# Hypergraph block on one core: second batch's degrees and B stage ahead of the first W2 stage, zero matmuls ahead of the first A, edge means ahead of z

## The reference

```python
h = relu(layernorm(x))                       # 1024 x 256
H = (adj != 0);  w = adj[0, :]               # incidence; first row = hyperedge weights
Dn = 1 / (H @ w);  Be = 1 / H.sum(axis=0)    # node degrees, edge counts (0 where empty)
z = relu(Dn * (H @ (Be * (H.T @ (h @ W1.T)))) + b1)
z = layernorm(z) * gamma + beta              # 1024 x 512
y = Dn * (H @ (Be * (H.T @ (z @ W2.T)))) + b2
out = x + (y + h)
```

## Time and profile before

| | us |
|---|---|
| median of 3 runs | 637.7 (637.48 to 640.55) |
| the profiled execution's own time | 639.25 |
| its span, first to last instruction | 637.4 |
| busy: PE / DVE / ACT / POOL | 620.3 / 473.3 / 290.9 / 111.6 |
| mean granted TensorE clock | 0.997 |

### The profile page before, as it was taken

One profiled execution on the slowest core, in us unless ns is written; L12 is line 12 of the kernel. 1 busy time (PEld: TensorE's weight loads), 2 busy tenths in 40 slices (PEclk: granted clock), 3 DMA queues, 4 the chain that ended last, 5 costly groups with the idle time before them and its releaser, 6 DMA issues.

```text
span 637.4 us, 11994 instructions
## 1 busy us (share of the span) xinstructions
PE 620.3 (97%) x4808; PEld 467.7 (73%) x4808; DVE 473.3 (74%) x1148; ACT 290.9 (46%) x540; POOL 111.6 (18%) x132
## 2 busy tenths in 40 slices
PE   2999899999999999999999999999999999999998
PEld 2756758688586885778766886768858688586887
DVE  6999878976599665995779948798478876388632
ACT  4476743463435535364353632646334363125620
POOL 0115029230310304004040040401212012000000
PEclk9999989999999999999999999999999999999999
DMA  8995870069800697109940099203990159000701
GB/s 336 260 348 105 143 320 4 31 144 179 339 34 1 160 201 301 34 1 204 258 201 34 26 222 299 116 34 84 205 364 10 34 111 213 9 1 2 197 3 67
DMA packets 146215, 89.78 MB, mean 141 GB/s; under 512 B 134896, under 2 KB 135536, under 8 KB 141168
## 3 DMA queue, kind: packets, MB, share of 16 engines
q1 hardware_dynamic: 146160, 89.02, 51.8%
HBM read 47.06 MB, written 8.39 MB: 87 GB/s over the span
## 4 chain that ended last, share of the span: by engine, by line
PE 90%; DVE 6%; ACT 2%; DMA 1%; issue 0%
PE acc L583 18%; PE acc L600 18%; PE acc L523 15%; PE acc L564 12%; PE acc L544 11%; PE acc L503 7%; PE acc L505 7%; PE acc L485 2%; DVE z L940 1%; DMA z<-z_split_ring 1%; DVE incidence L876 1%; DVE stat L945 1%; DMA x_in<-x 1%; ACT z L673 1%; ACT z_split_ring L672 1%; ACT residual L649 1%
## 5 line engine op out<-in xcount | busy, mean ns | idle before, releaser
L583 PE MATMUL acc<-xw_split,incidence 128*128 128x256 f16 x1024 | 113.2, 273 | 0.0
L600 PE MATMUL acc<-edge_means,incidence_t 128*128 128x256 f16 x1024 | 113.1, 273 | 0.0
L583 PEld LDWEIGHTS acc<-xw_split,incidence 128*128 128x128 bf16 x1024 | 100.1, 98 | 13.2 <-DVE xw_split L976 0.2
L600 PEld LDWEIGHTS acc<-edge_means,incidence_t 128*128 128x128 bf16 x1024 | 100.2, 98 | 13.1
L630 ACT ACTIVATE edge_means<-acc,edge_inverse 128x256 f16<-128x256 f32 x128 | 55.4, 474 | 116.8 <-PE acc L583 69.9
L503 PE MATMUL acc<-h_split,incidence 128*128 128x257 f16 x448 | 98.6, 273 | 0.0
L505 PE MATMUL acc<-h_split,incidence 128*128 128x256 f16 x448 | 98.6, 273 | 0.0
L523 PE MATMUL acc<-incidence_t,edge_means 128*128 128x512 bf16 x448 | 97.8, 379 | 0.0
L564 PE MATMUL acc<-w_split,z 128*128 128x256 f16 x768 | 87.2, 276 | 2.2 <-DMA z<-z_split_ring 2.2
L564 PEld LDWEIGHTS acc<-w_split,z 128*128 128x128 f16 x768 | 75.8, 99 | 12.3 <-issue 2.5
L544 PE MATMUL acc<-w_split,pt_split 128*128 128x512 f16 x384 | 84.2, 379 | 0.0
(11 more groups left out here) (104 smaller groups left out, 636.9 us busy)
## 6 DMA issues: line engine op xcount, KB each, us to landing
adj_in<-adj SPq DMA_DIRECT2D x32, 1024.0 KB, 10.4
out<-residual SPq DMA_DIRECT2D x32, 256.0 KB, 2.6
x_in<-x SPq DMA_DIRECT2D x7, 1024.0 KB, 5.5
edge_weights<-adj SPq DMA_DIRECT2D x7, 512.0 KB, 3.7
x_in<-x SPq DMA_DIRECT2D x2, 512.0 KB, 4.5
z<-w1t SPq DMA_DIRECT2D x1, 512.0 KB, 12.5
xw_split<-w2t SPq DMA_DIRECT2D x1, 512.0 KB, 13.3
incidence_t<-incidence SPq DMA_TRANSPOSE x32, 4.9
```

Of the source, the lines that this page charges most:

```text
L583: last = nc.tensor.matmul(acc[:, 0:DOUT], inc[:, b.slot, ct, P * et:P * (et + 1)], xw[:, ct, part, :], start=(ct == 0 and part == HI), sto ...
L600: last = nc.tensor.matmul(acc[:, 0:DOUT], inc_t[:, b.slot, ct, et, :], edge[:, et, part, :], start=(et == 0 and part == HI), stop=(et == T ...
```

## The change

Five edits, all in the opening; the loop from its second pass on is unchanged.

1. `keep_busy`: POOL clears the high half and low half of the first edge tile (`zeros_set`), and TensorE runs 22 matmuls of 512 columns on these zeros into the last bank, released by the first half of x, ahead of `first_stage_a`.
2. On DVE `split_weights` and the largest of gamma times W2 move from ahead of the first edge means to behind them; the first weight factor (`factor(0, ...)`) moves behind the second batch's x statistics. On ACT the W1 copies move behind the square root for x and the first two B drains.
3. The weight columns of two batches are loaded and split, and the second batch's degrees are 64 more matmuls on TensorE (`first_degrees(Batch(0, 1))`, `degrees_from_bank`), ahead of B(1); its DVE degree instructions and its load of the weight row fall away.
4. On TensorE the first pass is degrees, B(1), D(0), E(0) in place of D(0), B(1), E(0). Banks, drains and waits follow (`place`; D's upper half waits for B's drains, `pt_ready`; `first_stage_e` takes the first two edge tiles together and their last node tile last). On DVE and ACT `phase_b(1, 2)` comes ahead of `phase_d(0)`, the third batch's upper h0 tiles behind it.
5. On ACT and DVE the second batch's edge means come in two runs of four ahead of most of z's split, and the third batch's x statistics and square root stand among the z tiles. On SP the third batch's x load comes after the first z transpose.

```diff
             elif stage == "B":
-                at = T if first else 4 * T + 4 + PER_BATCH * (k - 1)
+                at = T if first else 3 * T + 4 if opening else 4 * T + 4 + PER_BATCH * (k - 1)
...
-                at = 3 * T + 4 + PER_BATCH * k - (T if last else 0)
+                at = 4 * T if first else 3 * T + 4 + PER_BATCH * k - (T if last else 0)
...
-            load_edge_weights(nxt)
...
             for q in range(QUARTERS):
+                if q == 1:
+                    load_x(Batch(0, 2))
                 sp.wait_ge(zs_ready, QT * (q + 1))
                 transpose_z(b0, q)
-            load_x(Batch(0, 2))
...
+            nc.gpsimd.memset(edge[:, 0, :, :], 0.0).then_inc(zeros_set, 1)
...
+            def keep_busy():
+                pe.wait_ge(zeros_set, 1)
+                pe.wait_ge(x_first, 16)
+                for _ in range(BUSY):
+                    nc.tensor.matmul(acc_ring[:, RING - 1, :], edge[:, 0, HI, 0:P],
+                                     edge[:, 0, :, :], start=True, stop=True)
...
-            def first_degrees():
-                pe.wait_ge(col_step, 5)
+            def first_degrees(b):
+                if b.offset == 0:
+                    pe.wait_ge(col_step, 5)
+                else:
+                    pe.wait_ge(t1_ready, b.count(T, DEGREE_BANK - place("A", b, 0) + 1))
+                    for q in range(QUARTERS):
+                        pe.wait_ge(inc_t_ready[q], b.count(16, 16))
...
-                    if not (isinstance(b.loop, int) and b.offset == 0):
+                    if b.offset > 1:
                         pe.wait_ge(xf_ready, b.next(-1).count(T, j + 1))
+                    if b.offset == 1 and place("B", b, j) == DEGREE_BANK:
+                        pe.wait_ge(deg_read, 2)
...
+                    elif b.offset == 0 and t >= T // 2:
+                        pe.wait_ge(pt_ready, b.next(1).count(4, t + 1 - T // 2))
                     else:
-                        pe.wait_ge(t1_ready, b.next(1).count(T, t + 1))
+                        pe.wait_ge(t1_ready, b.next(1).count(T, T if b.offset == 0 else t + 1))
...
+            def first_stage_e():
+                b = Batch(0, 0)
+                order = [(et, ct) for et in (0, 1) for ct in range(T - 1)] + [(0, T - 1), (1, T - 1)]
+                order += [(et, ct) for et in range(2, T) for ct in range(T)]
+                for et, ct in order:
+                    if ct == 0:
+                        pe.wait_ge(xf_ready, b.count(T, et + 1))
+                    if et == 0:
+                        pe.wait_ge(xw_ready, b.count(T, ct + 1))
...
+            keep_busy()
             first_stage_a()
...
+                if n == 0:
+                    first_degrees(Batch(0, 1))
+                    stage_b(Batch(0, 1))
+                    stage_d(Batch(0, 0))
+                    first_stage_e()
+                else:
+                    stage_d(Batch(0, n))
+                    stage_b(Batch(0, n + 1))
+                    stage_e(Batch(0, n))
...
+            root_x(b1_)
+            drain_b(b0, 0)
+            drain_b(b0, 1)
             act.wait_ge(w1_scale, 5)
             copy(w1s[:, :, HI, :], w1f, scale=wr[:, 2:3])
             copy(w1f, w1f, scale=wr[:, 2:3]).then_inc(w_hi, 1)
-            root_x(b1_)
-            drain_b(b0, 0)
-            drain_b(b0, 1)
```

More of the change, by code:

```diff
@@ L586, in stage_e @@
                     last.then_inc(e_done, 1)
+            def first_stage_e():
[7 more added lines that the diff above has]
+                        pe.wait_ge(xw_ready, b.count(T, ct + 1))
+                    acc = bank("E", b, et)
+                    for part in (HI, LO):
+                        last = nc.tensor.matmul(acc[:, 0:DOUT], inc[:, b.slot, ct, P * et:P * (et + 1)],
+                                                xw[:, ct, part, :],
+                                                start=(ct == 0 and part == HI), stop=(ct == T - 1 and part == LO))
+                    if ct == T - 1:
+                        last.then_inc(e_done, 1)
             def stage_f(b):
@@ L686, in phase_b @@
                 if bx is not None:
-                    root_x(bx)
+                    if b.offset > 1:
+                        root_x(bx)
                     h0_tiles(bx, 0)
@@ L691, in phase_b @@
                 drain_b(b, 1)
-                if bx is not None:
+                if b.offset == 1:
+                    h0_hi_part(bx, 1)
+                elif bx is not None:
                     h0_hi_part(bx, 1)
@@ L697, in phase_b, with upper_h0 @@
                 drain_b(b, 2)
-                if bx is not None:
+                if bx is not None and b.offset > 1:
                     h0_hi_part(bx, 3)
                 drain_b(b, 3)
+            def upper_h0(bx):
+                h0_tiles(bx, 2)
+                h0_tiles(bx, 3)
+                h0_hi_part(bx, 2)
+                h0_hi_part(bx, 3)
             def z_relu_tile(b, t):
@@ L791, in _ @@
             z_relu_tile(b0, 7)
+            for et in range(T // 2):
+                t1_hi_part(b1_, et)
             z_split(b0, 2)
@@ L795, in _ @@
             z_split(b0, 3)
-            t1_hi_part(b1_, 0)
-            t1_hi_part(b1_, 1)
+            for et in range(T // 2, T):
+                t1_hi_part(b1_, et)
             z_split(b0, 4)
             z_split(b0, 5)
-            t1_hi_part(b1_, 2)
-            t1_hi_part(b1_, 3)
             z_split(b0, 6)
+            root_x(Batch(0, 2))
             z_split(b0, 7)
-            for et in range(T // 2, T):
-                t1_hi_part(b1_, et)
             for n in range(N - 2):
-                phase_d(Batch(0, n))
+                if n > 0:
+                    phase_d(Batch(0, n))
                 phase_b(Batch(0, n + 1), Batch(0, n + 2))
+                if n == 0:
+                    phase_d(Batch(0, 0))
+                    upper_h0(Batch(0, 2))
                 phase_e(Batch(0, n))
@@ L915, in phase_b @@
             def phase_b(b, bx, bi=None):
-                if bx is not None:
+                if bx is not None and b.offset > 1:
                     x_stats(bx)
                 b_lo(b, 0)
+                if bx is not None and b.offset > 1:
+                    inverse_root(x_ln, x_step, bx, X_STEPS, 1.0)
                 if bx is not None:
-                    inverse_root(x_ln, x_step, bx, X_STEPS, 1.0)
                     if bi is not None:
@@ L931, in phase_b @@
                         incidence(bi, 3)
-                    h0_lo(bx, 2)
+                    if b.offset > 1:
+                        h0_lo(bx, 2)
                 b_lo(b, 2)
-                if bx is not None:
+                if bx is not None and b.offset > 1:
                     h0_lo(bx, 3)
@@ L1102, in _ @@
                     t1_lo_part(b0, et)
-            factor(0, w1_scale, 1.0 / (H0_SCALE * PT_SCALE * W_SCALE))
+            dve.wait_ge(gamma_w2, 1)
+            largest(1, gf).then_inc(max_here, 1)
+            split_weights()
             x_stats(nxt)
             inverse_root(x_ln, x_step, nxt, X_STEPS, 1.0)
+            factor(0, w1_scale, 1.0 / (H0_SCALE * PT_SCALE * W_SCALE))
             b_lo(b0, 0)
@@ L1151, in _ @@
             z_lo(b0, 0)
+            edge_inverse(nxt, 0)
             z_stats(b0, 7)
+            for et in range(T // 2):
+                t1_lo_part(nxt, et)
+            variance(z_ln, z_stat, z_step, b0, Z_STEPS, DH, upper)
             z_lo(b0, 1)
-            variance(z_ln, z_stat, z_step, b0, Z_STEPS, DH, upper)
-            z_lo(b0, 2)
-            edge_inverse(nxt, 0)
             inverse_root(z_ln, z_step, b0, Z_STEPS, ZN_SCALE, upper)
-            z_lo(b0, 3)
-            t1_lo_part(nxt, 0)
-            t1_lo_part(nxt, 1)
             dve.wait_ge(w2_scale, 5)
```

60 lines of the change are left out of this document (34 added, 26 removed).

## The result

| | before | after |
|---|---|---|
| median of 9 runs, us | 637.50 | 636.17 |
| lowest to highest, us | 637.05 to 640.55 | 635.18 to 636.68 |
| ratio of the times | | 0.996, 95% interval 0.9944 to 0.9977 |
| profiled execution: time, span, us | 639.25, 637.4 | 636.17, 634.4 |

By the ratio of the times the changed kernel is 0.4% faster, by the two medians 0.2% (1.33 us). 636.17 lies inside the predicted range (632.9 to 637.0), 1.4 us above the predicted 634.8 and 0.4 above the forecast's own range; it is close to the time of rival (a), 636.4. The nine times of the changed kernel form two groups, four at 635.2 to 635.4 and five at 636.2 to 636.7; the profiled one is of the second group.

What follows compares the result with a forecast made beforehand. TensorE, busy 620.3 of 637.4 us, was taken as the bound. Terms -1.55 + 1.61 - 4.20 + 0.2 = -3.9 from the profiled 639.25 gave 635.3, set to 634.8 for faster runs having less to gain; range 632.9 to 637.0.

Steps and rivals of the forecast that it cites:

- forecast's own range: Whole kernel: 634.0 to 635.8 us around the forecast of 634.8, given a chance of 0.55.
- rival (a): Opening: the clock falls before the first A or the zeros overrun its start; loses 1.55, giving 636.4 us; chance 0.14.
- Zeros and edge means: Opening: zeros end near 11.1 so A runs warm, and earlier edge means let B start at 25.95: -1.55 us.
- DVE's margins: Opening: DVE's pair behind B's drains has 0.7 us to spare, its last incidence tiles 0.9; neither holds TensorE.
- Degrees: Second batch: 64 narrow matmuls, none hidden, add 1.61 us to TensorE; taking the degrees off DVE gains nothing.
- B ahead of D: First pass: D finds its z when it starts, removing the wait and the slow clock behind it: -4.20 us.
- B's wait: Second batch's B waits for its edge means: +0.2 us, between 0 and 1.5.
- Sum: All terms together: -3.9 us from the profiled execution's 639.25, giving 635.3.
- signs that the prediction named: TensorE: zeros until about 11.1, A's last matmul near 25.5, B at 26.0, first E near 93.5, no 0.50 clock after 12.
- rival (c): First pass: the third batch's x load lands late and D waits, despite 4.0 us to spare; about 641 us, chance 0.04.

## Why the prediction was right or wrong

- **Zeros and edge means, -1.55 predicted, -0.6 measured.** This is the step that failed. The prediction took 7 slow zeros, the length of A's slow part, and let 22 zeros end at 11.1. It was 13 in the profile (8 to 14 over all traces), and they ended 0.9 us after A could start. That is rival (a) in part, whose sentence that 1 us more at the low clock costs only 0.5 was right, only that it was 2.6 us more. With 16 zeros the term is -1.48 (27.50 to 26.02), so the mechanism and its full size stand. That both edits are needed is shown: the zeros without the new order give B no earlier start (27.55 in before with 22 zeros), nor does the new order without zeros (27.93).
- **DVE's margins, 0.7 and 0.9.** TensorE did not wait for B's drains (pt) or for incidence, but the pt pair ended at 48.9, not 47.6, and the last incidence pair at 53.9, not 52.6: POOL's subtraction, which the prediction never looked at, now lay beside the first incidence pair and took 1.7 us from VectorE. Half a microsecond of margin was left there (A of the second batch starts at 54.41).
- **Degrees, +1.61.** 1.62 measured (68.43 to 70.05), and again for the second pass. The predicted zero for VectorE's side was wrong: with the degrees back there the kernel was 2.4 us slower. With the pass made twice the clock fell, so the price holds for one pass.
- **B ahead of D, -4.20, and B's wait, +0.2.** The wait for z and the lower clock are gone from the changed kernel. B paused once, 0.14 us behind its matmul at 71.56, when it came to the fifth edge tile, too short for the table. With the degrees the three terms add up to -2.39, and the traces give 26.07 - 28.53 = -2.46. So the mechanism and the size hold against that profile; a usual execution of before has less to lose, as the next points say.
- **Sum.** -3.9 from the profiled execution, measured -3.1 at the second C and in the whole time. The difference is the zeros' 0.9. Of the signs that the prediction named, no wait of TensorE above 0.5 us, one pass of narrow matmuls and no lower clock came true; A's last matmul, B and E came 0.9 to 1.0 later than named, and the zeros' end 1.4.
- **From profile to median.** Taken from the profiled execution, the sum was 635.3; with the zeros' 0.9 that is 636.2, and 636.17 was measured. So the 0.5 that the prediction took off towards the median, to reach 634.8, went the wrong way. Rival (a)'s 636.4 comes near the measured time partly by luck: it loses the whole 1.55, where 0.9 was lost, but from a sum that stands 0.5 too low. The guess behind the choice, that part of the spread is slow stretches of which faster executions have less, fits the times: a quarter of before's executions had a lower mean clock and took 2.3 us more. The median gained 1.3 us against 3.1 in the profiles. An estimate from the medians: without zeros and with the old means 0.9 was gained with 1.6 of degrees paid, so D's stall is worth about 2.6 us in a usual execution of before, not 4.2.
- **x load, rival (c).** It did not come, but the margin was about 2.2 us and not 4.0, and what waits is E for the W2 drains. In one execution of a kernel without zeros the load did land after 8.2 us and cost E 0.9.

Two things stay open. Kernels without zeros spread over 1.3 to 3.6 us, those with 16 over 0.2 to 0.8. POOL's late start and x's landing can be parts of it, and A's own slow part is another: in the six traces without zeros its last matmul lies between 26.91 and 27.43. Why POOL started late is not known; it did so with 22 zeros too (0.6 us of C, in the profile with the x load later). And no profile shows an execution of before at the full clock, so how long D waits there is seen only in the kernel with zeros added (0.82).

## What to carry to other kernels

Where an engine's first stage is slow because it starts cold, work ahead of it can warm it up, but how much is slow varies from trace to trace (8 to 14 zeros of the same size). Size the filler by the slowest case seen, so that it ends ahead of the real work: idle times of 0.18 to 1.29 us behind it cost no pace here, while whatever runs past the release of the real work is lost in full. An earlier producer is worth nothing until the consumer's engine is free at that time; look at what stands in its queue. And a profile is one execution: before a stall is put into the sum, compare the profile's own time and clock with those of the other executions, and add the sum to the time that it was read from.

## What the runs showed of the hardware

The lower clock can follow a stretch in which TensorE was never idle: the 128 matmuls of 3 columns were followed by the 1.2 GHz level in the profile (0.50 from 72 to 75 us); 64 of them were not, in any trace. After idle times it came behind one of 2.22 and one of 2.29 us (before), and in a row of four of 0.47 us each, from 97.0 to 100.1 (the x load later), but not in the traces with single pauses of 0.82 (before with zeros) or 2.12 us (after without zeros).

The granted clock does not show the slow start. In the changed kernel 12 of the 22 zeros took from 4.92 to 9.99, 0.42 us each, as the timeline from 9.99 on shows, while the windows there read 1.00:

```profile
9.99 2.65 PE L440 MATMUL acc<-edge_means 128*128 128x512 f16 x10
```

```profile
6.00:8.00 2.00, 2.00 (x6) 1.00 1.02 414
8.00:10.00 2.00, 2.00 (x7) 1.00 0.97 410
```

The slow pace at the start is read from the spacing of the matmuls.

The same x load of 1 MB took 4.9 to 8.2 us to land in the fourteen traces. The order on SyncE does not settle it: behind the first transpose alone it took 5.5 to 8.2.
